# First batch of the last attention prepared through seven PSUM banks, partly ahead of the top-k stage's last product

## What is computed

```python
# sixth layer (top-k feed-forward), B = 8 batches of 256 tokens
z = layernorm(x) @ ternary(W_syn).T + b_syn          # 2048 per token
thresh = top_k(z, 204)[..., -1:]
hidden = where(z >= thresh, relu(z), 0)
x = x + tanh(g) * layernorm(xn + hidden @ ternary(W_out).T + b_out)   # xn = layernorm(x); gamma, beta
# seventh layer (attention with a context), per batch
q = rope(rms_norm(xn @ wq)); k = rope(rms_norm(xn @ wk)); v = xn @ wv
k_ctx = rms_norm(ctx @ wk_ctx); v_ctx = ctx @ wv_ctx
out = softmax(q @ concat(k_ctx, k).T * scale + causal) @ concat(v_ctx, v)
x = x + tanh(g) * (out @ wo)
```

## Time and profile before

| | us |
|---|---|
| median of 3 runs | 3602.38 (3601.9 to 3604.39) |
| profiled execution | 3601.69 |
| its span | 3599.9 |
| TensorE busy | 2964.1 (82%) |
| VectorE busy | 2606.7 (72%) |
| ScalarE busy | 1641.7 (46%) |
| GpSimd busy | 872.3 (24%) |

### The profile page before, as it was taken

How to read it: one execution, slowest core, us unless ns; L and a number is a source line. 1 busy time by engine, 2 the same in 40 slices (tenths; PEclk the granted TensorE clock), 3 DMA queues, 4 the chain that set the end, 5 groups by cost and what they waited for, 6 DMA issues and landing times.

```text
span 3599.9 us, 50392 instructions
## 1 busy us (share of the span) xinstructions
PE 2964.1 (82%) x18610; PEld 1735.8 (48%) x18610; DVE 2606.7 (72%) x4530; ACT 1641.7 (46%) x2565; POOL 872.3 (24%) x1293
## 2 busy tenths in 40 slices
PE   3899899884668888578788745899999999998898
PEld 1343476663334444256566522444444444444565
DVE  4799769999756666588888874677777777776333
ACT  3000044444335555138778862444444444455343
POOL 2454200000000000015666682222222222221000
PEclk8899999997879999799989967999999999999999
DMA  7222022212211010200000021000000000012000
GB/s 263 83 79 76 27 59 71 59 48 71 54 24 30 22 24 10 97 30 2 1 1 2 4 87 53 7 7 1 7 7 1 7 7 1 7 37 61 13 17 17
DMA packets 52642, 132.51 MB, mean 37 GB/s; under 512 B 6416, under 2 KB 19536, under 8 KB 51152
## 3 DMA queue, kind: packets, MB, share of 16 engines
q1 hardware_dynamic: 43216, 96.11, 8.7%
q10 hardware_dynamic: 9216, 33.56, 3.1%
HBM read 119.03 MB, written 4.19 MB: 34 GB/s over the span
## 4 chain that ended last, share of the span: by engine, by line
PE 37%; DVE 17%; issue 10%; ACT 7%; POOL 1%; DMA 0%; DVEq 0%; SPq 0%; POOLq 0%; ACTq 0%
PE psum L1093 11%; PE psum L2392 3%; PE psum L1904 3%; PE psum L2433 3%; ACT area_g L1982 2%; PE psum L2417 2%; DVE area_c L2035 2%; PE psum L1918 2%; PE psum L1315 2%; PE psum L1334 2%; PE psum L2402 2%; DVE area_a L1651 2%; PE psum L1294 1%; PE psum L1939 1%; DVE small L2671 1%
## 5 line engine op out<-in xcount | busy, mean ns | idle before, releaser
L1982 ACT ACTIVATE area_g<-area_a 128x2048 bf16<-128x2048 f32 x156 | 310.6, 1995 | 43.7 <-DVE area_a L2053 30.2
L1904 PE MATMUL psum<-area_c,ident_bf 128*128 128x128 bf16 x3584 | 245.1, 232 | 100.3 <-DVE area_c L2035 100.3
L2671 DVE TENSOR_REDUCE small<-psum 128x1 f32<-128x384 f32 (+1 forms) x256 | 159.1, 622 | 188.5 <-PE psum L2393 188.5
L515 PE MATMUL psum<-area_b,area_g 128*128 128x512 f32 x640 | 281.2, 599 | 16.0 <-DVE area_g L464 14.4
L172 POOL TENSOR_TENSOR rstd<-mean_var,eps_col 128x2 f32<-128x2 f32 x65 | 16.3, 251 | 1139.9 <-DVE mean_var L581 528.4
L1904 PEld LDWEIGHTS psum<-area_c,ident_bf 128*128 128x128 bf16 x3584 | 227.8, 105 | 129.6 <-DVE area_c L2035 122.9
L659 PE MATMUL psum<-xT_high,area_a 128*128 128x256 f16 x1024 | 237.8, 280 | 1.4 <-DVE xT_low L596 1.4
L659 PE MATMUL psum<-xT_low,area_a 128*128 128x256 f16 x1024 | 237.4, 280 | 0.0
L2392 PE MATMUL psum<-area_b,stage 128*128 128x512 f32 (+1 forms) x512 | 234.5, 540 | 0.0
L2543 ACT ACTIVATE area_g<-psum 128x384 f16<-128x384 f32 (+1 forms) x256 | 139.3, 544 | 168.7 <-PE psum L2402 166.7
L515 PEld LDWEIGHTS psum<-area_b,area_g 128*128 128x128 f32 x640 | 121.3, 192 | 175.2 <-issue 164.6
(11 more groups left out here) (394 smaller groups left out, 7548.6 us busy)
## 6 DMA issues: line engine op xcount, KB each, us to landing
stage<-in_w ACTq DMA_DIRECT2D x24, 512.0 KB, 4.3
stage<-in_w SPq DMA_DIRECT2D x24, 512.0 KB, 3.7
area_g<-in_toeplitz SPq DMA_DIRECT2D x32, 256.0 KB, 3.5
area_b<-in_ctxT SPq DMA_DIRECT2D x16, 512.0 KB, 3.9
area_b<-area_b SPq DMA_DIRECT2D x24, 256.0 KB, 3.7
x_stream<-in_x SPq DMA_DIRECT2D x4, 1024.0 KB, 8.9
area_c<-in_ctxT SPq DMA_DIRECT2D x4, 1024.0 KB, 15.4
area_g<-in_ctx SPq DMA_DIRECT2D x8, 512.0 KB, 5.2
```

The lines of the kernel that those rows point to most:

```text
L515: last = nc.tensor.matmul(psum[:, 4 * par + m, :], toep[:, par, (m - k) * P:(m - k + 1) * P], kv[:, par, k, :], start=(k == 0), stop=(k == m))
L1904: last = nc.tensor.matmul(psum[:, 1, t_ * P:(t_ + 1) * P], identb[:, :], above5[:, t_, c * P:(c + 1) * P], start=(c == 0), stop=(c == KE - 1))
L1982: nc.scalar.activation(junk5[t_], z5[b % 3][:, t_, :], ACT.Sign, bias=fine5[:, par, t_:t_ + 1], scale=-1.0, accum_out=signs5[:, t_:t_ + 1] ...
L2671: nc.vector.tensor_reduce(nmax6[:, n % 2:n % 2 + 1], psum[:, 2 + n % 2, 0:nk], AX.X, ALU.min).then_inc(sig("nmax6_ready"), 1)
```

## The change

Each edit, engine by engine:

- **Chunk splits.** All 16 chunks are split in period 8: chunk k - 1 at the end of step k for k = 1 to 9, then three chunks at step 10, two at 11, two at 12. The stage's loops end with period 8; what was in periods 9 and 10 is written out in straight order.
- **Context of batch 0.** It is loaded into one of the chunk buffers as soon as chunk 13 has been split.
- **Banks and buffers.** The eight results of batch 0 go to banks 0, 1, 2, 3, 4, 5, 6 and again 1. Keys 2 and 6 of batch 0 have a square and a normalised buffer of their own (`near_n6`, `near_r6`).
- **TensorE** projects values 1, 3 and keys 0, 2 of batch 0 after period 8, ahead of the transposes and products of batch 7. It then projects the context (4, 5), the first query, 6 and 7, with the transposes between them.
- **Batch 7's sum, scaling and finish** are interleaved with the preparation of batch 0 on VectorE and GpSimd.
- **w3_o.** Chunks 0 to 3 are split before unit 0, chunks 4 to 7 inside unit 0, one per head. The context of batch 1 is loaded after the last of them.

```diff
@@ sp_stage5
+            sp.wait_ge(sig("stage_free"), prep6[1][13][0] + 1)
+            sp.dma_start(first_ctx6, t["ctxT"][:, :, 0, :]).then_inc(sig("ctx_part_loaded"), 16)
@@ pool_stage5
-            for p in PERIODS:
+            for p in range(-1, B + 1):
...
+            for t_ in range(TT):
+                for part_ in range(3):
+                    finish(B - 2, t_, part_)
+                pool.wait_ge(sig("x5_added"), TT * (B - 2) + t_ + 1)
+                for part_ in range(2):
+                    residual(B - 1, t_, part_)
+            return y_root, finish
@@ pe_stage5
+            front_done(pe, 0, 0, 6)
+            pe.wait_ge(sig("top5_ready"), B)
+            pe.wait_ge(sig("z5_ready"), 8 * B)
+            for j in (1, 3, 0, 2):
+                pe.wait_ge(sig("stage_free"), prep6[1][13 if j in SELF else 1][0] + 1)
+                project_kv6(pe, 0, j)
+            turn(B - 1, 0)
+            turn(B - 1, 1)
+            for n in range(8):
+                if n < 6:
+                    turn(B - 1, n + 2)
+                out(B - 1, n)
@@ dve_stage5
+            CHUNKS5 = {k: (k - 1,) for k in range(1, 10)}
+            CHUNKS5.update({10: (9, 10, 11), 11: (12, 13), 12: (14, 15)})
...
-                    if p == B and 1 <= k < 13:
-                        split_chunk(dve, dc, prep6, k - 1)
-                    if p == B + 1 and 1 <= k < 5:
-                        split_chunk(dve, dc, prep6, k + 11)
-                    if p == B + 1 and k == 10:
-                        tables6(dve, dc)
...
+                    if p == B:
+                        for n in CHUNKS5.get(k, ()):
+                            split_chunk(dve, dc, prep6, n)
...
+            select(B - 1, 0)
+            select(B - 1, 1)
+            y_scale(B - 2, 1)
+            for n in range(8):
+                low(B - 1, n)
+            tables6(dve, dc)
+            return y_sum, y_scale
@@ shared
+        FIRST_BANK = (0, 1, 2, 3, 4, 5, 6, 1)
+        near_n6, near_r6 = [xn[:, 1, n, :].rearrange("p (h d) -> p h d", h=4) for n in range(2)]
@@ pool_stage6
+            y_root(B - 1, 0)
             key_chunk(0, 0)
+            y_root(B - 1, 1)
+            key_chunk(0, 2)
             query_chunk(0)
-            key_chunk(0, 2)
             front_rstd(pool, pc, 0, 1, 6)
             key_chunk(0, 4)
+            finish(B - 1, 0, 0)
             key_chunk(0, 6)
+            finish(B - 1, 0, 1)
+            finish(B - 1, 0, 2)
+            for part_ in range(3):
+                finish(B - 1, 1, part_)
@@ pe_stage6
+            pe.wait_ge(sig("ctx_part_low_ready"), B + TT)
+            project_kv6(pe, 0, 4)
+            project_kv6(pe, 0, 5)
+            pe.wait_ge(sig("stats5_ready"), TT * B)
+            project_q(0)
+            turn_k(0, 0)
+            project_kv6(pe, 0, 6)
+            turn_k(0, 2)
+            pe.wait_ge(sig("v6_ready"), 1)
+            project_kv6(pe, 0, 7)
+            turn_q(0)
+            project_q(1)
+            turn_k(0, 4)
+            turn_k(0, 6)
+            pe.wait_ge(sig("kT6_ready"), 1)
             turn_x(1, 0)
             turn_x(1, 1)
@@ act_stage6
             split_ctx(0)
+            act.wait_ge(sig("weights_ready"), 2)
+            key_in(0, 0)
+            key_in(0, 2)
+            value_in(0, 1)
+            value_in(0, 3)
+            query_in(0)
+            key_in(0, 4)
+            value_in(0, 5)
+            query_out(0)
+            key_in(0, 6)
+            value_in(0, 7)
+            for n in range(4):
+                output_high(n)
+            query_in(1)
             x_high(1, 0)
             x_high(1, 1)
...
                 exps(n)
+                if u == 0:
+                    output_high(4 + h)
@@ dve_stage6
             low_ctx(0)
+            y_sum(B - 1, 0)
             key_begin(0, 0)
+            y_sum(B - 1, 1)
             key_end(0, 0)
+            key_begin(0, 2)
+            y_scale(B - 1, 0)
+            value_low(0, 1)
+            key_end(0, 2)
             query_begin(0)
+            y_scale(B - 1, 1)
+            key_out(0, 0)
+            value_low(0, 3)
+            dve.wait_ge(sig("x5_added"), 2 * TT)
+            x_stats(1)
             query_end(0)
+            key_begin(0, 4)
+            key_out(0, 2)
+            x_scale(1)
+            value_low(0, 5)
+            key_end(0, 4)
+            key_begin(0, 6)
+            key_out(0, 4)
+            key_end(0, 6)
+            value_low(0, 7)
+            for n in range(4):
+                output_low(n)
+            key_out(0, 6)
             x_low(1, 0)
             x_low(1, 1)
             maximum(0)
...
+                if u == 0:
+                    output_low(4 + h)
                 turned_low(n)
```

More of the change, by code:

```diff
@@ L1994, in x_high @@
                                      ACT.Copy, scale=LN_SCALE).then_inc(sig("xT_high_ready"), 1)
-            for p in PERIODS:
+            for p in range(-1, B + 2):
                 for k in range(FINE):
@@ L2199, in build @@
         qT6 = stage[:, 1, :].rearrange("p (a h q) -> p a h q", a=2, h=4)
+        first_ctx6 = stage[:, 1, :].rearrange("p (k s) -> p k s", k=KD)
         p6 = xn[:, 1]
@@ L2215, in sp_stage6 @@
             sp.wait_ge(sig("y5_ready"), TT * B)
[L2216 to L2220, removed]
+            for j, pas, k, c in prep6o[1]:
+                load_chunk(sp, j, prep6o[0][k][0], c)
+            sp.wait_ge(sig("stage_free"), prep6o[1][-1][0] + 1)
+            for b in range(1, B):
                 if b >= 2:
@@ L2259, in build, with key_bufs, kv_bank, ctx_part6 @@
         SELF, CTX = (0, 2), (4, 6)
+        FIRST_BANK = (0, 1, 2, 3, 4, 5, 6, 1)
+        near_n6, near_r6 = [xn[:, 1, n, :].rearrange("p (h d) -> p h d", h=4) for n in range(2)]
+        def key_bufs(b, j):
+            return (near_n6, near_r6) if b == 0 and j in (2, 6) else (nk6, rk6)
+        def kv_bank(b, j):
+            return FIRST_BANK[j] if b == 0 else 0
+        def ctx_part6(b):
+            return first_ctx6 if b == 0 else kT6[:, b % 2, 0:2].rearrange("p n g k -> p (n g k)").rearrange("p (k s) -> p k s", k=KD)
+        def project6(out, x, name, cols):
+            for k in range(KD):
+                last = product3(out, (x[0][:, k], x[1][:, k]), (w6[name][0][:, k, cols], w6[name][1][:, k, cols]), k == 0, k == KD - 1)
+            return last
+        def tokens6(b, t_):
+            return [x[:, b % 2, :, t_ * P:(t_ + 1) * P] for x in (xTh, xTl)]
+        def project_kv6(pe, b, j):
+            x = tokens6(b, (j // 2) % 2) if j < 4 else [split6[:, b % 2, (j // 2) % 2, v] for v in range(2)]
+            name = ("w3_k", "w3_v", "w3_k", "w3_v", "w3_kc", "w3_vc", "w3_kc", "w3_vc")[j]
+            project6(psum[:, kv_bank(b, j), :], x, name, slice(0, D)).then_inc(sig("v6_ps_ready" if j % 2 else "k6_ps_ready"), 1)
         chunk_no = {}
         def number_chunks():
-            order = [("k", 0, 0), ("q", 0), ("k", 0, 2), ("k", 0, 4), ("k", 0, 6)]
+            order = [("k", 0, 0), ("k", 0, 2), ("q", 0), ("k", 0, 4), ("k", 0, 6)]
             for u in range(UNITS):
@@ L2330, in pe_stage6 @@
         def pe_stage6(pe):
-            pe.wait_ge(sig("weights_ready"), 2)
-            def project(out, x, name, cols):
-                for k in range(KD):
-                    last = product3(out, (x[0][:, k], x[1][:, k]), (w6[name][0][:, k, cols], w6[name][1][:, k, cols]), k == 0, k == KD - 1)
-                return last
-            def tokens(b, t_):
-                return [x[:, b % 2, :, t_ * P:(t_ + 1) * P] for x in (xTh, xTl)]
             def project_kv(b, j):
-                t_ = (j // 2) % 2
                 if j == 0:
@@ L2350, in project_kv @@
                     pe.wait_ge(sig("ctx_part_low_ready"), B + TT * (b + 1))
-                x = tokens(b, t_) if j < 4 else [split6[:, b % 2, t_, v] for v in range(2)]
-                name = ("w3_k", "w3_v", "w3_k", "w3_v", "w3_kc", "w3_vc", "w3_kc", "w3_vc")[j]
-                project(psum[:, 0, :], x, name, slice(0, D)).then_inc(sig("v6_ps_ready" if j % 2 else "k6_ps_ready"), 1)
+                project_kv6(pe, b, j)
             def turn_k(b, j):
```

90 lines of the change are left out of this document (28 added, 62 removed).

## The result

The changed kernel takes 3555.49 us (median of 4 runs, 3551.15 to 3557.76) against 3602.88 before (4 runs, 3601.9 to 3604.39); the ratio is 0.9868, 95% interval 0.9853 to 0.9884. Forecast were 3556.4 us, a gain of 46; measured are 47.4. The profiled execution is the fastest of the four: 3551.15 us, span 3549.4.

A forecast was written before the change was run, and what follows sets the result against it. No engine was the bound, but a serial chain through PSUM bank 0. Gains 48.5 + 0 + 0 - 2.5 = 46 us off 3601.69, plus 0.7 for the median, gave 3556.4 us (own range 3549 to 3564).

The forecast's parts named there:

- One bank's circle: Batch 0's eight projections and four key transposes all pass PSUM bank 0, each waiting for copies; rounds of about 16 us.
- L: End of the last of eight low parts of the last batch's hidden values, 2161.9 us in the profile before.
- Part 1: Seven banks and projections ahead, between L and the loop's first maximum: 45 us against 93.5, a gain of 48.5.
- VectorE's unchanged list: VectorE's instructions between L and the first maximum, without four w3_o splits moved to unit 0: 38.3 us busy.
- Part 2: Key weights split in the last search: select about 6 us later, change of L 0 us, bounds -4 and +10.
- rows 5: Profile rows of VectorE and GpSimd side by side in the last search, used to price the moved splits.
- Part 3: 48 projection matmuls queued on TensorE before the last batch's transposes: cost 0, bound +2.
- Part 4: Four high and four low parts of w3_o moved into unit 0: cost 2.5 us, bounds 0 and 5.
- Rival 3: TensorE at half clock becomes the bound, before and after L: gain 30, 3572 us; chance 0.14.
- Rival 2: Dense splits make the last search and keys' projection late, L 6 to 10 later: gain 38, 3564 us; chance 0.17.
- Rival 1: VectorE isn't stretched between L and the first maximum, and L comes 3 us earlier: 3548 us; chance 0.14.
- Rival 4: VectorE and GpSimd exclude each other, VectorE's SBUF instructions take double everywhere: 10 us slower, 3612; chance 0.03.

The follow-up runs named there:

- the short finish: The changed kernel with GpSimd's three finishing steps of batch 7 done on 8 of 512 columns, the others left out; 3555.27 us (one run).
- the projections behind: The changed kernel with keys 0, 2 and values 1, 3 projected behind the last product of the top-k stage instead of ahead of its transposes; 3565.91 us.
- the two kernels that keep before's loop: The kernel before with only all 16 chunks split in period 8, 3600.62 us; the kernel before with only the banks and their TensorE order, 3573.81 us.
- the run with all splits ahead: The changed kernel with all eight w3_o chunks split before unit 0 and none in it; 3562.7 us, ratio 0.9883.

## Why the prediction was right

Point by point, in its own steps.

- **The reading of the profile** held. One bank's circle was the bound: the banks alone take 28.5 us out of the stretch from L to the first maximum. The orders, the projections ahead and the four w3_o splits that went to unit 0 take the other 21.
- **Part 1, the term that carried the sum:** 45 us forecast, 44.0 and 44.1 measured. The way to it, VectorE's unchanged list (38.3) plus waits plus more stretching, is right as a mechanism: with less for VectorE to do the stretch shrinks by as much (39.1 against 39.4 expected). The list measures 40.8 busy. The w3_o splits alone exceed it by more than the whole excess of 2.5, 8.3 us for four instead of 5.0, and the short finish shows that GpSimd's finishing steps cause most of it (8.3 becomes 5.9). I had placed the 3.3 us of stretching over ten encounters; it sits in the four splits (3.3), the x scaling (0.9) and the last key's scaling (1.0), while elsewhere the new order has less of it than before (the context's two low parts 1.4 us instead of 2.4). That the size came out right within 1 us is partly this cancelling, so partly luck. The waits were 3.2 where I had put 3.4 (44.0 less 40.8), of which 1.9 at x's second tile.
- **Part 2** came out near 0 for L (+0.3 and +0.8), but not by the cause that I put first. With the 3.2 us by which this execution began its search earlier added, VectorE is free at 2138.2, the threshold comes at 2139.1 and L is at 2162.2. I had VectorE free at 2139.6, the threshold at about 2138 and L at 2162. I had miscounted in rows 5: the split at 2117.53 is chunk 9's, and in the changed kernel too seven were left then and not eight. The search, slowed by the splits, is what sets select: VectorE waits 0.9 us for the threshold. The amount (+5.4 against my +5.8) is the right one for the wrong last arrival. The run without splits shows the mechanism: 58.9 us, at ScalarE's own pace. From select to the first low part I forecast 7 less and 5.4 came, since I had put the one scaling there at 0.6 us and left out its wait for GpSimd's root.
- **The page's rule** in part 2 (exclusive use of the shared port, "SBUF — State Buffer", section "Who interferes with whom", in the Trainium skill) was weighed as nearly neutral. The runs show that the slowing it speaks of decides this stretch: 10 us of the search, and 4.3 us between L and the first maximum by the short finish. The trace agrees with the rule where GpSimd's instructions end with VectorE's. The VectorE instructions with one input in SBUF and one in PSUM (L2751, mean 0.74 us, 0.75 before) weren't stretched.
- **Part 3** cost nothing, as said. The keys' 24 matmuls ran from 2127.0 to 2134.3, 1.6 us before select. With the projections behind, the kernel is 9.5 us slower by its stretches, 7.6 of it from L to the first maximum, so this part of the change is worth up to a fifth of the gain. It holds only as long as chunk 13 is split in time: without splits in the search the same queue held the transposes up. I had priced only what it costs and not what it saves by itself.
- **Part 4:** 2.5 forecast; 0.2 and 2.0 measured against before, 1.3 and 3.1 against the two kernels that keep before's loop, 0.9 and 2.7 against the run with all splits ahead. The size depends on TensorE's clock in unit 1, 1.00 or 0.91. I had all four splits in unit 0; the last one stands in unit 1's first head and costs 0.7 there at the same full clock. The second context's load behind the last split cost nothing that could be told from that.
- **The rivals.** Rival 3 (TensorE at half clock) showed once, in the first round of turn and out (3.38 us for 8 matmuls); from the next on it ran fast, and the mean clock from L was 0.84. Rival 2's mechanism was real, and one of its signs came, comparisons more than 3 us apart (4.0, 5.7 and 4.0); its 6 to 10 us at L did not, since select to first low part balances them. Rival 1 falls: the splits and scalings were stretched. Rival 4 would have needed doubling everywhere. Single instructions do double and more (a split's first half 0.75 to 1.55 us, the last key's scaling 0.68 to 1.68), and rows 5 already had 1.44 against 0.75 where I wrote 1.7 times; but the list as a whole grew from 38.3 to 40.8.

What stays open is why the clock of the coarse search, which the change doesn't touch, comes out differently from one execution to the next.

## What to carry to other kernels

When every engine is half idle, look for a resource that all results share, here one PSUM bank, and price the new way by the longest single engine's list with its waits: that list was the time within 1 us here, in part because errors cancelled. Work moved under "idle" VectorE time beside GpSimd isn't free; in this kernel GpSimd advanced by one instruction per VectorE split instruction, and 16 splits cost its search 10 us. So price the moved work with that, and prefer gaps where GpSimd has no chain to carry: four such instructions and the tables cost at most 0.6 us there. Ask too what a queue holds up when its input comes late, as the projections ahead of the transposes did. Gains of 5 us in a kernel of 3550 that spreads by 6 are seen in stretches measured from an event ahead of the change, not in totals.

## What the runs showed that was not expected

- The two profiled executions of the changed kernel differ ahead of the changed code by more than behind it, and the difference seen is in a search loop whose folds of 32 matmuls take 1.96 or 3.59 us. The mean clock from 1500 to 1800 us was 0.92 and 0.88. The change between the two lengths happens within one execution too. Behind it, the stretches repeat within 0.3 us apart from the first units.
- GpSimd's steps of three instructions with 1 column each can hold up a ScalarE comparison by 3.7 us when VectorE runs dense instructions on SBUF beside them (comparisons 5.7 us apart instead of 2.0).
